# A new slot order for the last chunk of a macaron block, with nine states instead of six read out on GpSimd

## What is computed

```
def ffn(x):                       # 512 -> 2048 -> 512
    return (silu(x @ wu.T) * (x @ wg.T)) @ wd.T
def mamba(resid):                 # E = 1024 channels, N = 16 states
    r = rmsnorm(resid) * norm_w
    skip, x = r @ W_skip, silu(causal_conv4(r @ W_in) + conv_b)
    delta = softplus(x @ W_delta_1 @ W_delta_2 + b_delta_2)
    Bm, Cm = x @ W_B, x @ W_C
    h[l] = h[l-1] * exp(delta[l] * A) + (delta[l] * x[l]) * Bm[l]
    y[l] = sum over n of h[l, :, n] * Cm[l, n]
    return resid + ((y + x * W_D) * silu(skip)) @ W_out
x = x + 0.5 * ffn(layernorm(x))
x = x + mamba(layernorm(x))
x = x + 0.5 * ffn(layernorm(x))
```

## Time and profile before

| | |
|---|---|
| median of three runs | 2800.42 us (2798.09 to 2802.14) |
| profiled execution | 2798.09 us, its span 2796.2 us |
| TensorE busy | 2614.3 us, 93% |
| VectorE busy | 2447.7 us, 88% |
| GpSimd busy | 2382.1 us, 85% |
| ScalarE busy | 1879.0 us, 67% |

### The profile page before, as it was taken

One profiled execution on the slowest core, in us unless ns is written; L12 is line 12 of the kernel. 1 busy time (PEld: TensorE's weight loads), 2 busy tenths in 40 slices (PEclk: granted clock), 3 DMA queues, 4 the chain that ended last, 5 costly groups with the idle time before them and its releaser, 6 DMA issues.

```text
span 2796.2 us, 51718 instructions
## 1 busy us (share of the span) xinstructions
PE 2614.3 (93%) x17439; PEld 2021.6 (72%) x17439; DVE 2447.7 (88%) x3221; ACT 1879.0 (67%) x4340; POOL 2382.1 (85%) x2023
## 2 busy tenths in 40 slices
PE   5776899999999999999999999999999999999878
PEld 4555677777878777786777778677777877776655
DVE  4378899999999999899999999899999999999892
ACT  7374867676676767667676766767676676767651
POOL 1168899999898999999998999999999898999881
PEclk9898999999999999999999999999999999999989
DMA  7013222223222322222232222222222222222220
GB/s 274 31 55 72 60 61 76 56 58 83 59 74 60 80 50 65 77 63 73 58 81 53 70 69 63 73 63 75 54 72 66 66 69 65 73 57 68 64 55 8
DMA packets 94446, 192.44 MB, mean 69 GB/s; under 512 B 12588, under 2 KB 32232, under 8 KB 93672
## 3 DMA queue, kind: packets, MB, share of 16 engines
q0 software_dynamic: 20304, 73.93, 13.7%
q1 hardware_dynamic: 73880, 115.21, 13.0%
HBM read 106.26 MB, written 8.91 MB: 41 GB/s over the span
## 4 chain that ended last, share of the span: by engine, by line
POOL 41%; PE 32%; issue 12%; DVE 7%; ACT 2%; DMA 1%; POOLq 1%; DVEq 0%; ACTq 0%
POOL h L778 22%; PE ps L1596 10%; POOL h L795 7%; PE ps L1607 6%; PE ps L1619 6%; POOL hl L884 4%; PE ps L1553 4%; PE ps L1668 4%; DVE h L1342 3%; POOL u L892 2%; POOL delta L849 2%; DVE xc L1400 1%; PE ps L1629 1%; POOL h L784 1%; POOL xw L799 1%
## 5 line engine op out<-in xcount | busy, mean ns | idle before, releaser
L778 POOL TENSOR_TENSOR h<-u,bb 128x1024 f32<-128x1024 f32 x512 | 1257.8, 2466 | 27.2 <-DVE u L1417 14.2
L1342 DVE TENSOR_TENSOR_SCAN h<-ps,h 128x512 f32<-128x512 f32 x1024 | 1191.8, 1207 | 36.5 <-POOL h L784 18.6
L1037 ACT ACTIVATE ps<-delta,a_neg 128x255 f32<-128x255 f32 x2048 | 873.1, 468 | 377.0 <-DVE h L1342 374.8
L1596 PE MATMUL ps<-xh,q_up 128*128 128x256 f16 x2048 | 466.5, 275 | 36.1 <-DVE xl L1280 19.1
L1364 DVE SCALAR_TENSOR_TENSOR y<-ps,ccur,y 128x512 f32<-128x512 f32 x678 | 471.4, 738 | 6.9 <-PE ps L1553 6.3
L1596 PE MATMUL ps<-xh,q_gate 128*128 128x256 f16 x2048 | 462.7, 273 | 8.1 <-DVE xw L1433 7.8
L1596 PE MATMUL ps<-xl,q_up 128*128 128x256 f16 x2048 | 466.5, 275 | 0.0
L1596 PE MATMUL ps<-xl,q_gate 128*128 128x256 f16 x2048 | 462.4, 273 | 0.0
L1553 PE MATMUL ps<-ident,h 128*128 128x128 f32 x2968 | 398.2, 277 | 50.2 <-DVE y L1364 46.7
L1553 PEld LDWEIGHTS ps<-ident,h 128*128 128x128 f32 x2968 | 344.6, 142 | 112.7 <-issue 50.9
L884 POOL TENSOR_TENSOR hl<-act,hh 128x512 f16<-128x512 f32 x256 | 314.5, 1229 | 97.3 <-ACT hh L1064 94.4
(11 more groups left out here) (126 smaller groups left out, 3642.9 us busy)
## 6 DMA issues: line engine op xcount, KB each, us to landing
xw<-h POOLq DMA_DIRECT2D x141, 512.0 KB, 4.5
bb<-b_scratch SPq DMA_DIRECT2D x224, 256.0 KB, 3.1
cplane<-c_scratch SPq DMA_DIRECT2D x141, 128.0 KB, 3.1
xs<-in_L_attn_resid_dram SPq DMA_DIRECT2D x17, 512.0 KB, 3.5
out_dram<-xs SPq DMA_DIRECT2D x15, 512.0 KB, 4.3
wraw<-in_L_ffn_W_up_dram SPq DMA_DIRECT2D x4, 1024.0 KB, 9.6
wraw<-in_L_ffn_W_gate_dram SPq DMA_DIRECT2D x4, 1024.0 KB, 12.3
wraw<-in_L_ffn_W_down_dram SPq DMA_DIRECT2D x4, 1024.0 KB, 14.1
```

The lines of the kernel that those rows point to most:

```text
L778: ins = pl.tensor_tensor(hs, u[:, :, :], bb[:, q % 2, s % PLANES:s % PLANES + 1, :].broadcast_to([P, HE, CH]), ALU.mult)
L1037: ins = ac.activation(abar[r][:, e, 1:], delta[:, k, 1:], ACT.Exp, scale=a_neg[:, k, n:n + 1])
L1342: v.tensor_tensor_scan(hr, abar[r].rearrange("p e t -> p (e t)"), hr, 0.0, ALU.mult, ALU.add).then_inc(scanned, 1)
L1596: ins = te.matmul(pp[:, f * CH:(f + 1) * CH], w[:, d, col:col + P], part[:, d, :], start=(d == 0 and part is xh), stop=(d == DB - 1 and pa ...
```

## The change

The lists of the last pass and of the drain are replaced, and the last chunk uses the elem set of the loop: nine states instead of six. Nothing else changes.

```diff
--- before.py
+++ after.py
@@ -165,36 +165,36 @@
 ]
 LAST_SLOTS = [
     [("OM_0", 0, 3)],
-    [],
-    [("OM_1", 0, 3)],
-    [("OM_1", 3, 4), ("OM_0", 3, 4), "D2_2"],
-    ["D2_3"],
+    [("OM_0", 3, 4)],
+    [],
+    ["D2_2", ("OM_1", 0, 1)],
+    ["D2_3", ("OM_1", 1, 4)],
     ["YT_2", "YT_3"],
-    [("OM_1", 4, 6)],
-    [("OM_0", 4, 6)],
-    [("OM_0", 6, 8), ("OM_1", 6, 8), ("SK_0", 0, 1)],
-    ["T2_0", ("SK_0", 1, 2)],
+    [("OM_0", 4, 5), ("OM_1", 4, 5)],
+    [("OM_0", 5, 6), ("OM_1", 5, 6), ("OM_0", 6, 7)],
+    [("OM_0", 7, 8), ("OM_1", 6, 8), ("SK_0", 0, 1)],
+    [],
     ["T2_1"],
-    [("SK_1", 0, 2)],
-    [("SK_2", 0, 1), "U2_0"],
-    ["G2_0", "U2_1"],
-    [("SK_2", 1, 2), ("SK_3", 0, 1)],
-    ["G2_1", ("SK_3", 1, 2)],
-    ["U2_2", "G2_2", "U2_3"],
-    ["G2_3"],
+    ["T2_0", ("SK_0", 1, 2), ("SK_1", 0, 2)],
+    ["U2_0", ("SK_2", 0, 1)],
+    ["G2_0", ("SK_2", 1, 2)],
+    ["U2_1"],
+    ["G2_1", ("SK_3", 0, 1)],
+    ["U2_2", "G2_2"],
+    ["U2_3", ("SK_3", 1, 2), "G2_3"],
     ["U2_4", "G2_4"],
     ["U2_5", "G2_5"],
-    ["YT_0"],
-    ["YT_1"],
-    ["U2_6", "G2_6"],
-    ["U2_7", ("DN2_0", 0, 6)],
-    [("DN2_1", 0, 1), "G2_7"],
-    [],
-    [("DN2_0", 6, 8), ("DN2_1", 1, 6)],
-    [("DN2_0", 8, 15), ("DN2_1", 6, 11)],
-    [],
-    [("DN2_1", 11, 15), ("DN2_0", 15, 16)],
-    [("DN2_1", 15, 16)],
+    [],
+    ["YT_0", "YT_1", "U2_6", ("DN2_0", 0, 1)],
+    ["G2_6", ("DN2_0", 1, 3)],
+    ["U2_7"],
+    ["G2_7"],
+    [("DN2_0", 3, 5), ("DN2_1", 0, 5)],
+    [("DN2_0", 5, 7), ("DN2_1", 5, 6), ("DN2_0", 7, 8)],
+    [("DN2_0", 8, 15), ("DN2_1", 6, 8)],
+    [("DN2_1", 8, 11)],
+    [("DN2_0", 15, 16), ("DN2_1", 11, 13)],
+    [("DN2_1", 13, 16)],
     [],
 ]
 DRAIN_SLOTS = [
@@ -202,33 +202,33 @@
     [],
     [],
     [],
-    [("OM_1", 0, 1)],
-    ["YT_2", "YT_3"],
+    ["YT_2"],
+    ["YT_3", ("OM_1", 0, 1)],
     [("OM_1", 1, 2), ("OM_0", 4, 5)],
-    [],
-    [],
     [("OM_0", 5, 8)],
-    [("OM_1", 2, 5)],
-    [],
-    [],
-    [("OM_1", 5, 8)],
+    [],
+    [],
+    [("OM_1", 2, 8)],
+    [],
     [],
     ["T2_0"],
-    ["T2_1", "U2_0"],
-    [],
-    [],
-    ["G2_0", "U2_1"],
-    ["G2_1"],
-    ["U2_2"],
+    [],
+    [],
+    ["T2_1"],
+    [],
+    ["U2_0", "G2_0"],
+    [],
+    ["U2_1"],
+    ["G2_1", "U2_2"],
     ["G2_2"],
     ["U2_3", "G2_3", "U2_4"],
-    [("DN2_0", 0, 3), "G2_4", ("DN2_0", 3, 4), "U2_5"],
-    [("DN2_0", 4, 6)],
-    ["G2_5", "U2_6", ("DN2_1", 0, 6)],
-    [("DN2_0", 6, 8)],
-    ["G2_6", ("DN2_1", 6, 10), "U2_7", "G2_7", ("DN2_0", 8, 9)],
-    [("DN2_0", 9, 12), ("DN2_1", 10, 13), ("DN2_0", 12, 16), ("DN2_1", 13, 16)],
-    [],
+    [("DN2_0", 0, 3), "G2_4", "U2_5"],
+    [("DN2_0", 3, 6), "G2_5"],
+    [("DN2_0", 6, 8), "U2_6"],
+    [],
+    ["G2_6", "U2_7", ("DN2_0", 8, 9), "G2_7"],
+    [("DN2_1", 0, 12), ("DN2_0", 9, 12)],
+    [("DN2_0", 12, 16), ("DN2_1", 12, 16)],
     [],
 ]
 UG = {k: {f"{x}{k}_{p}" for x in "UG" for p in range(PAIRS)} for k in (1, 2)}
@@ -268,7 +268,7 @@
 EDGES_AT = 0
 ELEM = [3, 9, 11, 15, 17, 18, 22, 27, 31]
 ELEM_FIRST = [3, 9, 11, 15, 17, 18, 22, 27, 31]
-ELEM_LAST = [5, 9, 11, 17, 23, 28]
+ELEM_LAST = [3, 9, 11, 15, 17, 18, 22, 27, 31]
 ELEM_PLANES = 4
 ELEM_AHEAD = 6
 EDGE_STEPS, RSTD_STEPS, RMS_STEPS = 5, 5, 11
```

More of the change, by code:

```diff
@@ L204 @@
     [],
-    [("OM_1", 0, 1)],
-    ["YT_2", "YT_3"],
+    ["YT_2"],
+    ["YT_3", ("OM_1", 0, 1)],
     [("OM_1", 1, 2), ("OM_0", 4, 5)],
+    [("OM_0", 5, 8)],
     [],
     [],
-    [("OM_0", 5, 8)],
-    [("OM_1", 2, 5)],
-    [],
-    [],
-    [("OM_1", 5, 8)],
-    [],
+    [("OM_1", 2, 8)],
+    [],
+    [],
     ["T2_0"],
-    ["T2_1", "U2_0"],
     [],
     [],
-    ["G2_0", "U2_1"],
-    ["G2_1"],
-    ["U2_2"],
+    ["T2_1"],
[4 more added lines that the diff above has]
+    ["G2_1", "U2_2"],
     ["G2_2"],
     ["U2_3", "G2_3", "U2_4"],
-    [("DN2_0", 0, 3), "G2_4", ("DN2_0", 3, 4), "U2_5"],
-    [("DN2_0", 4, 6)],
-    ["G2_5", "U2_6", ("DN2_1", 0, 6)],
-    [("DN2_0", 6, 8)],
-    ["G2_6", ("DN2_1", 6, 10), "U2_7", "G2_7", ("DN2_0", 8, 9)],
-    [("DN2_0", 9, 12), ("DN2_1", 10, 13), ("DN2_0", 12, 16), ("DN2_1", 13, 16)],
-    [],
+    [("DN2_0", 0, 3), "G2_4", "U2_5"],
+    [("DN2_0", 3, 6), "G2_5"],
+    [("DN2_0", 6, 8), "U2_6"],
+    [],
+    ["G2_6", "U2_7", ("DN2_0", 8, 9), "G2_7"],
+    [("DN2_1", 0, 12), ("DN2_0", 9, 12)],
+    [("DN2_0", 12, 16), ("DN2_1", 12, 16)],
     [],
```

## The result

After the change the kernel takes 2820.88 us (median of four runs, 2820.39 to 2822.42) against 2799.68 us before (four runs, 2798.09 to 2802.14): 1.0073 times as long, 95% interval 1.006 to 1.0084. It is slower, by 21.2 us. The forecast was 2813.8 with a range up to 2820.0: right in sign, 7.1 us short, and 0.9 us outside the range. The profiled execution took 2822.87 us. Eighteen more executions of the kernel after, taken beside the experiments, lie between 2816.37 and 2824.83 us with a median of 2819.7, so the 0.9 us by which the range was missed are within what executions differ by; the 7 us to the forecast are not.

What follows compares the result with a forecast made beforehand. GpSimd's products were taken to bound the last chunk's scan, with a serial drain after it. 11.3 (scan end) + 2.7 (state 31) + 1.7 (clock) = 15.7 us over 2798.1 gave 2813.8 us, range 2803.5 to 2820.

Steps and rivals of the forecast that it cites:

- The start-up delay: First stretch of chunk 15's scan: state 3's multiply ahead of rstd delays the chain behind it, 3.7 us late at u(16).
- The second stretch: u(16) to u(28): multiplies of 15 and 18 add 7.7 us, a 1.07 us DMA wait goes; delay reaches 10.3 us.
- The third stretch: Between u(30) and u(31): the multiply of state 27 adds 3.85 us, to 14.2 us late at the end of u(31).
- cover: Before scan(31): VectorE's lag of 2.9 us absorbs part of the delay, so the last scan's end T comes 11.3 us late.
- State 31 at the end: After the last scan's end T: y_plus_x waits for state 31's multiply and DMA landing, T + 7.9, 2.7 us more.
- TensorE's clock: Out projection behind the gate: a gap of about 4.3 us ahead of it brings a slower clock, costing 1.7 us.
- The drain lists: Drain from U2_0 to the end: TensorE has no gap there, so the new order wins nothing, 0 us.
- rival 1: Scan of the last chunk: GpSimd bound only by its own work, start-up delay taken back; 2805.2 us, chance 0.15.
- rivals 2 and 3: Last scan: VectorE sets the pace with less work, 2796.6 us (0.13, with all between); its gaps also close, 2790.9 us (0.07).
- rival 4: Last pass and drain: the lists do it all, the elem set being neutral; falls together with rival 2, no separate chance.

Runs made afterwards that it cites:

- e2: Kernel after with the old LAST_SLOTS and DRAIN_SLOTS, so the kernel before with the new nine-state elem set; ratio to before 1.0067.
- e1: Kernel after with the old elem set (5, 9, 11, 17, 23, 28), so only the new lists; ratio to before 1.0003.
- e6: Kernel after with slots 9 to 11 of the last pass put back (T2_0, T2_1 and SK pieces); ratio to before 1.006.
- e7: Kernel after with state 5 in place of state 3 in the elem set; ratio to before 1.0051.
- e11: Kernel after with rstd put ahead of the product in slot 8 of the last pass; ratio to before 1.0072.
- e5: Kernel before with state 31 in place of 28 in the elem set, old lists; ratio to before 1.0033.
- e12: Kernel before with only the drain list changed, pieces of OM_1 put ahead of the wait for the gate; ratio to before 0.9991.
- e13: Kernel before with the drain list of e12 and four elem states (5, 11, 17, 28) instead of six; ratio to before 1.0009.
- e14: Kernel before with the drain list of e12 and five elem states (5, 9, 17, 23, 28); ratio to before 0.9994.

## Why the prediction was wrong, point by point

**The start-up delay: the chain right, the bound wrong.** rstd ended 26.5 us after u(2) (the 2621.1 of the forecast is +26.9, counted from u(2) of before), normalise waited 5.90 (about 6), scan(7) came at +30.6 (2625.1 is +30.9). From there the step "In LAST_SLOTS the OM, SK and DN2 moves lie where TensorE has room: 0" failed. They lie there only as long as VectorE is on time. The forecast followed the delay through ScalarE and VectorE to the first hh, and did not ask whether TensorE would still free the ring of h. The first hl was forecast near 2647, which is +52.8; it came at +56.1. Of the missing 4.8 us, e2 shows 0.6 without the new lists, e1 shows 1.9 without the new set, of which up to 1.3 is scatter, and 2.3 are the two together; e6, e7 and e11 tie these to the lump and to state 3.

**The second stretch: right.** Two multiplies and one wait less were to give 6.6 us and gave 6.2; the six other kernels with 15, 17, 18 and 22 in their set gave 6.1. The wait of VectorE at y_plus_x for elem 15's DMA cost nothing, as the forecast had it.

**The third stretch: size right, cover wrong.** Elem 27 put 3.6 us between u(28) and u(31), and u(31) itself, behind its DMA issue, took 2.65 instead of 2.35 us; forecast 3.85 in all (its rows add up to 3.9). But "this lag of 2.9 us is cover" failed: u(31) to T shrank by 0.6 only. VectorE's timeline of the kernel after, which answers to the scans of the earlier trace rows:
```profile
2737.64 4.56 DVE L1342 TENSOR_TENSOR_SCAN h<-ps,h 128x512 f32<-128x512 f32 x4
2742.11 1.39 DVE L1364 SCALAR_TENSOR_TENSOR y<-ps,ccur,y 128x512 f32<-128x512 f32 x2
2743.41 2.33 DVE L1342 TENSOR_TENSOR_SCAN h<-ps,h 128x512 f32<-128x512 f32 x2
2745.66 1.38 DVE L1364 SCALAR_TENSOR_TENSOR y<-ps,ccur,y 128x512 f32<-128x512 f32 x2
2747.66 1.60 DVE L1364 SCALAR_TENSOR_TENSOR y<-ps,ccur,y 128x512 f32<-128x512 f32 x2 [0.61 <-PE ps L1553]
2753.76 1.29 DVE L1433 TENSOR_TENSOR xw<-ps,xw 128x512 f32<-128x512 f32 x2 [4.50 <-DMA xw<-h]
```
u(31) is ready at 2741.4 and scan(31) starts at 2743.41, so 2.0 of the 2.9 us of lag still stand. 28 has left the elem set, so its y addition (1.3 us, at 2742.11) now lies between scan(30) and scan(31), where before the two scans ran back to back. I had counted VectorE's work as 4.2 us less over the whole and not looked at which slot gets more. The rows behind 2700 us do show VectorE with gaps (one of 5.24 us at 2701.53), but not from 2721.87 on.

**State 31 at the end: right.** T to y_plus_x was to be 7.9 and was 8.0 in every kernel with the lists or set of after that has 31. The last chain of waits in the kernel after, which answers to the earlier trace rows:
```profile
2749.19 4.45 DMA xw<-h
...
2757.07 8.01 PE ps L1668 x18
...
2774.14 17.55 PE ps L1596 x144
...
2807.80 9.94 PE ps L1607 x46
```
The DMA took 4.45 us from issue to landing, and VectorE waited 4.50 for it. The estimate of 3.2 us by the Trainium skill, page "DMA: Bandwidth & Descriptors", section "Anatomy of one DMA", is too low for it: the trace shows 1.2 us more. No run here shows whether it is the accumulation that costs it.

**TensorE's clock: 0 instead of 1.7, the gap wrong.** TensorE's timeline of the kernel after:
```profile
2751.09 3.18 PE L1668 MATMUL ps<-w_out,gz 128*128 128x512 f32 x4
2755.85 9.22 PE L1668 MATMUL ps<-w_out,gz 128*128 128x512 f32 x20 [1.58 <-POOL gz L906]
```
The last row equals the 9.21 us of before. The step that failed is the gap of 4.3 us ahead of the gate: it was 1.58. The gate came when forecast (2755.85 is T + 10.1), but TensorE's work ahead of it ended at T + 8.5 instead of T + 5.7, since the half clock came earlier than forecast: 0.50 in 2748 to 2753 us, above. It fell on the transposes of y and on four records of OM ahead of the gate, which took 3.18 us (in the trace of before two pairs of them took 1.02 us each), and was over at 2753.8, ahead of the gate. In e2, e5, e6, e7 and e11 the clock fell at the gate a second time, and the same 20 records took 10.43 to 10.91 us. So 1.2 to 1.7 us, the forecast's size, show in those kernels and not in this one. "TensorE: Matmul & The Clock Gate" of the Trainium skill, section "Why this matters for your kernels", says that an idle gap between bursts puts the engine back to half rate; the trace agrees for the gap of 4.21 us ahead of the transposes at 2742.98, behind which the granted clock was 0.50. "Above zero for certain" did not follow, for the gap can be another than forecast, and the slow stretch can lie on work that has slack.

**The drain lists: right.** y_plus_x to the end was 67.3 us, forecast 67 to 69; 46 down matmuls in 9.94 us at the end instead of 28 in 6.06 changed nothing, since TensorE is full from U2_0 on. In sum the start gave +4.8 us, the cover +2.3, the second and third stretch -0.8, clock and drain -2.2 and the tail +0.1: 4.2 us. The profiled execution had 5.1 more ahead of u(2), and the median lies 2.0 below it; that makes the 7.1, but for rounding. The clock's 1.7 us were thus forecast and did not come, which hid as much of the start and of the cover: that the forecast was only 7.1 us short is in part luck.

**The rivals.** The start-up delay was not taken back (rival 1): in place of the old waits came 6.7 us of new ones. That VectorE sets the pace with less work (rivals 2 and 3) fell too: up to T VectorE had 2.6 us less work, and T came 17.6 us later. That the lists do it all (rival 4) is excluded by e1_lists_only.

## What to carry to other kernels

When an engine is made later, ask of every ring buffer behind it who frees it, and what bulk work an in-order queue holds in front of the small instruction that does so: a block of matmuls that fits a gap today is in the way when its neighbour slips. And a lag counted as cover must be re-counted in the slots where it lies, since an edit that takes work off an engine in total can put some of it in exactly that place.

## What the runs showed of the hardware that was not expected

The granted clock can fall twice within a few microseconds, and the second fall is what costs. In e7_elem5_for_3 it was at half until 2744.5, back at full while TensorE idled ahead of the gate (2747.81), and at half again from 2748.0 to 2751.4, on the out projection. Four stretches of e7_elem5_for_3, and then two of the kernel after, whose gate came at 2755.85:
```profile
2741.50:2744.50 3.00, 3.00 (x10) 2.23 (x10) 0.00 (x0) 0.00 (x0) 0.52 (x1) 0.50 0.69 135
2745.00:2747.80 2.80, 0.71 (x2) 0.00 (x0) 1.29 (x2) 0.00 (x0) 1.30 (x2) 1.00 0.01 0
2748.00:2751.00 3.00, 3.00 (x4) 1.11 (x4) 0.00 (x0) 0.00 (x0) 0.98 (x1) 0.50 0.00 0
2752.00:2755.00 3.00, 3.00 (x8) 1.33 (x7) 1.39 (x2) 0.00 (x0) 0.00 (x0) 1.00 0.00 0
```
```profile
2750.00:2753.00 3.00, 3.00 (x10) 1.97 (x9) 0.00 (x0) 0.00 (x0) 0.06 (x1) 0.50 0.89 173
2754.00:2757.00 3.00, 1.39 (x3) 0.30 (x2) 1.05 (x2) 0.00 (x0) 2.46 (x2) 1.00 0.00 0
```
What sets the kernels apart is TensorE's gap right ahead of the gate. It was 0.83 us in before, 1.58 in after and 1.69 in e12, e13 and e14, and in all five the out projection ran at full clock, in 0.46 to 0.47 us a record. It was 1.93, 2.10, 2.31, 3.79 and 4.60 us in e11, e7, e6, e2 and e5, and in all five the clock fell to 0.50, between 0.2 us ahead of the gate and 1.4 us behind it. No run changed this gap alone, so that it is the cause is not shown. It moves the total by 1.2 to 1.7 us, and so is part of why the gains at T of e6 and e11 (3.3 and 2.6 us) are not fully seen in their totals.
